# One group of the output projection in each chunk of the next round

## The chip, the cores and the metric

The kernel runs on one core of one Trainium2 chip. The metric is the time of one execution in microseconds of the device, as the median of several runs. The engines named below are TensorE (PE, with its weight loads as PEld), VectorE (DVE), ScalarE (ACT), GpSimd (POOL) and SyncE (SP), which only issues transfers.

## The reference, cut to what matters

The whole program is a decoder-like stack of two layers, each an attention part and a feed-forward part, every part followed by a sum with its input and a layer norm. The change is in the first part alone, a chunked linear attention with decay over 2 sequences of 1024 tokens, width 512, 16 heads of 32:

```python
q, k, v = silu(x @ Wq), silu(x @ Wk), silu(x @ Wv)     # split into 16 heads of 32
def step(S, inp):                                      # one chunk of 128 tokens
    scores = einsum('bchd,bshd->bhcs', qb, kb) * D
    o_intra = einsum('bhcs,bshd->bchd', scores, vb)
    o_inter = einsum('bchd,bhde->bche', qb, S) * q_decay
    S_new = chunk_decay * S + einsum('bshd,bshe->bhde', kb * k_decay, vb)
    return S_new, o_intra + o_inter
o = o * sigmoid((x @ Wg1) @ Wg2)
o = head_rmsnorm(o) * norm_w
x = layernorm(x + o @ Wo)
```

The last line's `o @ Wo` is the output projection ("wo" in the kernel), and `x + ...` the addition that goes with it.

## The kernel before, in words

Features lie on partitions, 4 pieces of 128, and tokens along the free axis. The 2048 tokens are cut into tiles of 512 (`TT`), a tile into four chunks of 128 (`CPT` = 4). The attention phase is five rounds: rounds t = 0 to 3 take tile t, and a tail round finishes tile 3. Every engine has its own program, a loop of `body(rd)` over the rounds, and the programs meet only at semaphores, so the order of the code within each engine is the order of its work.

A product in full precision is three matmuls in a reduced format: weights and data are split into a high part (a rounding copy, by ScalarE) and a low part (the rest, by GpSimd or VectorE), and `three_passes` (L111 to L113) multiplies high by high, high by low and low by high. A projection group of 128 output features over 512 tokens (`project`) is 4 x 3 = 12 matmuls into one of two PSUM banks (`proj`). The groups of all rounds stand in the lists `FIRST`, `SECOND`, `NEXT` and `TAIL`; `s_pj` counts finished groups, and `taken` says which engine has to have read the group two places before.

TensorE's round t: (from t = 2 the mean of an older tile, `mean_parts`, L369, which waits for the additions of tile t - 1 to x), then q (4 groups), `transform(0)` (L407, a step of the transform of the feed-forward weights, which waits for GpSimd's butterflies), the head norms of the tile before (L395), k, the gate's first product (L417), v, the gate (L520), `transform(1)`, four transposes of k (L525), the output projection of the tile BEFORE (`outputs`), and last the four chunks. In a chunk: `scores_of` (L430, 16 matmuls of 32 rows), `from_state` (L445, 16 of 32 x 32 into `o_ps`), `state_update` (L454, 16 of 32 columns into `u_ps`), `from_chunk` (L464, 16 of 32 columns into `o_ps`). `from_chunk(c)` waits until VectorE has masked the four score banks (`s_pr`), and `from_state(c + 1)` until VectorE has gated chunk c (`s_og`).

VectorE's round ends with four reads of the transposes (L858), four additions of the projection to x (`add_outputs`, L824), and for each chunk: four maskings (L868), the state (L872, four small instructions) and the gating (L877).

Three things hang on the last group of the output projection:

- The projection's inputs `onh` and `onl` are the buffers `xh` and `xl`, which hold the high and low part of the tile's x in the next round. So ScalarE's next round begins with

```python
act.wait_ge(s_pj, rd.base)
act.copy(xh[:, :, :], x[:, :, tok(t)]).then_inc(s_xh, 1)     # L629
```

  where `rd.base` is the number of all groups of the rounds before, the last `wo` among them.
- GpSimd's next round waits for that copy (`pool.wait_ge(s_xh, rd.t + 1)`), makes the four low parts (L739), then the low parts of three blocks of later weights (`blocks_low`, L719, behind ScalarE's L579), then eight butterflies (L732, L733). TensorE's q waits for all four low parts (`pe.wait_ge(s_xl, KD * t + 1)`), and `transform(0)` for the butterflies (`s_bf`).
- In the tail round ScalarE makes the high parts of the first feed-forward tile after the same count (`ffn_x_high`, L638), then two of weights (L632) and two blocks; GpSimd follows with the low parts of the data (L749) and of the weights (L753). TensorE's tail begins with `first_ffn_chunk(0)` (12 matmuls), which waits for them (`joint.lo13`, `joint.xl`), and goes on with the head norms, `first_ffn_chunk(1)` and the output projection of tile 3.

SyncE stores the blocks as GpSimd finishes them (L305) and loads the next ones (L300). The second phase of the kernel begins when all engines have left the block of the first.

Of the kernel before, what the change touches and what calls it, by code (L numbers as in the profile page):

```python
# [26 lines left out]
ALU = mybir.AluOpType  # L27
# [4 lines left out]
KD = D // P  # L32
# [72 lines left out]
def tok(t):  # L105
    return slice(t * TT, (t + 1) * TT)
# [9 lines left out]
def attention_phase(nc, joint, w13a, en, cn, w13b, w13x, x_dram, aw_d, ld_tok, ld_feat, ld_cols, wg1_d, wg2_d, nw_d, w2n, w2h):  # L116
# [6 lines left out]
    with ExitStack() as ctx:  # L123
# [4 lines left out]
        x, qT, aw_hi, aw_lo = joint.x, joint.first, joint.hi, joint.lo  # L128
# [25 lines left out]
        onh, onl = xh, xl  # L154
# [17 lines left out]
        s_pj = p.sem("proj_done")  # L172
# [11 lines left out]
        s_oh, s_ol = p.sem("on_hi"), p.sem("on_lo")  # L184
# [73 lines left out]
        with nc.Block() as block:  # L258
# [83 lines left out]
            def _(pe):  # L342
                def body(rd):
# [9 lines left out]
                    def project(name, w, m, hi, lo, ready=None):  # L353
                        out = bank(name, m)
                        for k in range(KD):
                            if ready is not None:
                                for sem, value in ready(k):
                                    pe.wait_ge(sem, value)
                            mm = three_passes(pe, out, aw_hi[:, w, k, m * P:(m + 1) * P],
                                              aw_lo[:, w, k, m * P:(m + 1) * P],  # L360
                                              hi[:, k, :], lo[:, k, :], k == 0, k == KD - 1)
                        mm.then_inc(s_pj, 1)
# [31 lines left out]
                                pe.wait_ge(*by_piece(m, s_sq, NT, p_sq))  # L394
                            pe.matmul(bank("norm", m), const[:, C_HEAD:C_HEAD + P], sq[:, m, :]).then_inc(s_pj, 1)  # L395

                    def outputs():
                        for m in range(KD):
                            project("wo", 3, m, onh, onl, (lambda k: [(s_ol, KD * rd.prev + k + 1)]) if m == 0 else None)

                    def transform(i):

# [45 lines left out]
                    def state_update(c):  # L448

                        pe.wait_ge(*rd.out("kT", c))  # L450
                        for m in range(KD):
                            for j in range(HPT):
                                hs = slice((m * HPT + j) * HD, (m * HPT + j + 1) * HD)
                                mm = pe.matmul(u_ps[j * HD:(j + 1) * HD, m, :], kd[:, c, hs], v[:, c, hs],  # L454
                                               tile_position=(0, j * HD))
                        mm.then_inc(s_u, 1)
# [22 lines left out]
                    if rd.tail:  # L479
                        first_ffn_chunk(0)  # L480
                        norms()
                        first_ffn_chunk(1)
                        outputs()
                        return
                    if rd.norms_x:
                        mean_parts()
# [35 lines left out]
                    for c in range(CPT):  # L522
# [2 lines left out]
                            mm = pe.transpose(out[:, m * P:(m + 1) * P], kT[:, m, c * CH:(c + 1) * CH],  # L525
                                              const[:, C_ID:C_ID + P])
                        mm.then_inc(s_pj, 1)
                    if not rd.first:
                        outputs()
                    scores_of(0)  # L530
                    for c in range(CPT):
                        from_state(c)
                        state_update(c)
                        from_chunk(c)
                        if c + 1 < CPT:
                            scores_of(c + 1)
# [221 lines left out]
            def _(dve):  # L758
# [28 lines left out]
                def body(rd):  # L787
                    t = rd.t

                    def norm_heads():  # L790

                        dve.wait_ge(s_og, CPT * t)
                        for m in range(KD):
                            dve.wait_ge(s_sd, KD * rd.prev + m + 1)
                            dve.scalar_tensor_tensor(out=on[:, m], in0=og[:, m, :], scalar=nw[:, m:m + 1],
                                                     in1=sq[:, m], op0=ALU.mult, op1=ALU.mult).then_inc(s_on, 1)

                    def centre_x():

                        dve.wait_ge(s_pj, rd.done("mb"))  # L800
                        for k in range(KD):
                            xt = x[:, k, tok(t - 2)]
                            dve.tensor_tensor(xt, xt, rd.bank("mb"), ALU.subtract)\
                               .then_inc(s_dt if k == KD - 1 else s_lc, 1)

                    def scale_x():

                        dve.wait_ge(s_lr, t - 1)
                        for k in range(KD):
                            xt = x[:, k, tok(t - 2)]  # L810
                            dve.tensor_tensor(xt, xt, lsq[:, 0], ALU.mult).then_inc(s_ln, 1)

                    def low_of_normed():

                        for k in range(KD):
                            dve.wait_ge(s_oh, KD * rd.prev + k + 1)
                            dve.tensor_tensor(onl[:, k], on[:, k], onh[:, k].bitcast(F32), ALU.subtract).then_inc(s_ol, 1)

                    def add_outputs():

                        for m in range(KD):
                            dve.wait_ge(s_pj, rd.done("wo", m))
                            xt = x[:, m, tok(rd.prev)]
                            dve.tensor_tensor(xt, xt, rd.bank("wo", m), ALU.add).then_inc(s_dt, 1)  # L824

                    if rd.tail:
                        norm_heads()
                        low_of_normed()
                        dve.wait_ge(joint.th, 1)
                        dve.scalar_tensor_tensor(out=ffn_sg, in0=ffn_sg, scalar=1.0, in1=joint.gate[:, :],  # L830
                                                 op0=ALU.add, op1=ALU.mult).then_inc(joint.sg, 1)
                        add_outputs()
                        return
                    if rd.norms_x:
                        centre_x()
                    dve.wait_ge(*rd.out("q", KD - 1))
                    dve.tensor_tensor(qd[:, :, :].rearrange("p m (c i) -> p m c i", c=CPT),
                                      qT[:, :, :].rearrange("p m (c i) -> p m c i", c=CPT),
                                      qdec[:, :, :].unsqueeze(2).to_broadcast([P, KD, CPT, CH]),
                                      ALU.mult).then_inc(s_qd, 1)  # L840

                    if not rd.first:
                        dve.wait_ge(s_st, (CPT + 1) * t)
                    dve.tensor_tensor(st[:, :, :].rearrange("p m c -> p (m c)").bitcast(I32),
                                      st[:, :, :].rearrange("p m c -> p (m c)").bitcast(I32),
                                      live[:, t:t + 1].to_broadcast([P, KD * HD]),
                                      ALU.bitwise_and).then_inc(s_st, 1)
                    if not rd.first:
                        norm_heads()
                    if rd.norms_x:  # L850
                        scale_x()
                    if not rd.first:
                        low_of_normed()
                    if rd.norms_x:
                        dve.wait_ge(s_ln, KD * (t - 1))
                    for c in range(CPT):
                        dve.wait_ge(s_pj, rd.done("kT", c))
                        dve.tensor_tensor(kd[:, c, :], rd.bank("kT", c), kdec[:, :], ALU.mult)\  # L858
                           .then_inc(s_dt, 1)
                    if not rd.first:  # L860
                        add_outputs()
                    dve.wait_ge(*rd.out("gate", KD - 1))
                    dve.wait_ge(s_st, (CPT + 1) * t + 1)
                    for c in range(CPT):
                        n = CPT * t + c
                        for j in range(HPT):
                            dve.wait_ge(s_sc, HPT * n + j + 1)
                            dve.tensor_tensor(pr[:, j], scores[j], dmask[:, j], ALU.mult).then_inc(s_pr, 1)  # L868

                        dve.wait_ge(s_u, n + 1)  # L870
                        for m in range(KD):
                            mm = dve.scalar_tensor_tensor(out=st[:, m], in0=st[:, m], scalar=cdec[:, m:m + 1],  # L872
                                                          in1=u_ps[:, m], op0=ALU.mult, op1=ALU.add)
                        mm.then_inc(s_st, 1)
                        dve.wait_ge(s_o, n + 1)
                        gated = sig[:, :, c * CH:(c + 1) * CH]
                        dve.scalar_tensor_tensor(out=gated, in0=gated, scalar=1.0, in1=o_ps[:, :, :],  # L877
                                                 op0=ALU.add, op1=ALU.mult).then_inc(s_og, 1)
                        dve.wait_ge(s_st, n + t + 2)
# [1137 lines left out]
```

## Time and profile before

| | |
|---|---|
| time of the kernel, median of 3 runs | 1880.44 us (1876.88 to 1881.67) |
| profiled execution, span from the first to the last instruction | 1871.9 us (its time as a run is not recorded apart; the median lies 8.5 us above the span) |
| busy | PE 1753.7 us (94%), PEld 1149.7 (61%), DVE 1323.0 (71%), ACT 982.2 (52%), POOL 1284.0 (69%) |
| attention phase | from 0 to about 360 us |
| an addition of the projection to x (L824, x16) | 686/689/689 ns (min/median/max) |
| loads of blocks after the chunks of round 1 (L300) | start at 156.03 us; ScalarE takes them from 191.10 (L579); 3.7 us each to landing |
| granted clock at 0.50 | seven stretches in which TensorE works; the shortest from 21.5 to 24.9 us, after 2.37 us without a matmul. In the one from 585.63, 512-column matmuls step 0.427 us (590.30, 590.73, 591.16). At 371 to 377 us the clock is 1.00 |

How to read it: times are from the span's start. A matmul's record is longer than its step, since matmuls are pipelined; steps are read from start to start. A row of a timeline has start, length, engine, line and operation, output and inputs, the count of instructions merged into it, and in brackets the idle time of the engine before it and what ended that. "issue" is time in which the engine waited for nothing that the profile shows. A row of the windows has the stretch, its length, then the busy time of PE, PEld, DVE, ACT and POOL with their instructions, the granted TensorE clock as a share of 2.4 GHz, the share of the DMA engines and GB/s.

### The profile page before, as it was taken

Reading aid. Unit: us, or ns where it says so; the run is one execution under the profiler, and the core shown is the slowest. Engines: PE = TensorE matmul, PEld = TensorE weight load, DVE = VectorE, ACT = ScalarE, POOL = GpSimd, SP = SyncE. Lnnn points to the kernel's source line nnn. Section 1 sums busy time; section 2 is a strip of 40 time slices with the busy share of each in tenths; the row PEclk is TensorE's granted clock in tenths of the full one; section 3 lists DMA queues with packets and bytes.
Section 4 is the critical chain, followed back from the end, with each engine's and each line's share of the span. In section 5 each row is a group of like instructions: output and inputs, shape, how many; then the busy total and the mean of one; then the engine's idle time right before and its main releaser. Section 6 shows DMA issues by size and latency. Waiting matters only on the chain. (4 is left out here: it accounts for less than half of the span.)

```text
span 1871.9 us, 27455 instructions
## 1 busy us (share of the span) xinstructions
PE 1753.7 (94%) x9472; PEld 1149.7 (61%) x9472; DVE 1323.0 (71%) x1532; ACT 982.2 (52%) x1686; POOL 1284.0 (69%) x992
## 2 busy tenths in 40 slices
PE   7898989799998999999899999999999999999998
PEld 5666666577755655555555556555556565667886
DVE  2424343433249989899998999899999999993322
ACT  5343443567465656755666556655554555543212
POOL 4533445166448998798987998798988798983111
PEclk9999999999999999999999999999999999999999
DMA  7442323588758888798787987686878687874662
GB/s 247 131 139 82 124 80 124 185 289 271 268 190 280 300 267 278 234 297 285 238 265 228 316 272 255 232 279 226 272 249 284 225 274 252 291 252 158 204 195 96
DMA packets 159226, 427.32 MB, mean 228 GB/s; under 512 B 30992, under 2 KB 54096, under 8 KB 158704
## 3 DMA queue, kind: packets, MB, share of 16 engines
q1 hardware_dynamic: 159088, 425.57, 68.7%
q8 instruction: 76, 1.25, 0.3%
q14 instruction: 62, 0.51, 0.1%
HBM read 356.30 MB, written 69.21 MB: 227 GB/s over the span
## 5 line engine op out<-in xcount | busy, mean ns | idle before, releaser
L1647 ACT ACTIVATE decay<-delta_on_states,a_neg 128x512 f32<-128x512 f32 x512 | 354.4, 692 | 339.3 <-DVE h_states L1803 338.2
L1898 POOL TENSOR_TENSOR q_or_raw_or_h_times_c<-h_states,c_rep 128x512 f32<-128x512 f32 x293 | 382.7, 1318 | 58.7 <-PE scan_y L1470 29.9
L1898 POOL TENSOR_TENSOR h_times_c_rest<-h_states,c_rep 128x512 f32<-128x512 f32 x219 | 283.5, 1304 | 36.0 <-DVE h_states L1803 17.9
L1864 POOL TENSOR_TENSOR h_lo<-v_or_silu_in_h_lo,h_hi 128x512 fp32r<-128x512 f32 x128 | 169.1, 1321 | 176.1 <-ACT h_hi L1545 172.3
L1803 DVE TENSOR_TENSOR_SCAN h_states<-decay,h_last,d_b 128x512 f32<-128x512 f32 x192 | 242.3, 1274 | 5.9 <-ACT decay L1647 1.1
L1803 DVE TENSOR_TENSOR_SCAN h_states<-decay,d_b 128x512 f32<-128x512 f32 x192 | 230.8, 1214 | 5.5 <-ACT decay L1647 1.2
L111 PE MATMUL y_or_aux<-h_hi,w 128*128 128x512 f32 x468 | 208.2, 445 | 5.8 <-POOL h_lo L1864 4.8
L1461 PE MATMUL du_spread<-stack,selectors 96*128 96x512 bf16 x512 | 159.0, 390 | 46.7 <-DVE d_b L1772 30.1
L1729 DVE SCALAR_TENSOR_TENSOR v_or_silu_in_h_lo<-v_or_silu_in_h_lo,gate_or_scores 128x512 f32<-128x512 f32 x127 | 86.3, 680 | 145.6 <-ACT v_or_silu_in_h_lo L1541 145.2
L112 PE MATMUL y_or_aux<-h_lo,w 128*128 128x512 f32 x468 | 184.7, 395 | 0.0
L113 PE MATMUL y_or_aux<-h_hi,w 128*128 128x512 f32 x468 | 184.1, 393 | 0.0
L1889 POOL TENSOR_TENSOR d_b_by_pool<-du_copied,b_rep 128x512 f32<-128x512 f32 x128 | 171.4, 1340 | 8.0 <-ACT du_copied L1655 8.0
L1772 DVE TENSOR_TENSOR d_b<-du_spread,b_rep 128x1024 f32<-128x1024 f32 x128 | 153.7, 1201 | 13.0 <-PE du_spread L1461 12.5
L1470 PE MATMUL scan_y<-q_or_raw_or_h_times_c,sum_selectors 128*32 128x512 f32 x586 | 135.8, 608 | 0.0
L111 PEld LDWEIGHTS y_or_aux<-h_hi,w 128*128 128x128 f32 x468 | 89.0, 190 | 73.1 <-issue 35.4
L1545 ACT CAST h_hi<-v_or_silu_in_h_lo 128x512 fp32r<-128x512 f32 x128 | 78.7, 615 | 101.2 <-DVE v_or_silu_in_h_lo L1735 100.9
L1735 DVE SCALAR_TENSOR_TENSOR v_or_silu_in_h_lo<-v_or_silu_in_h_lo,up_or_scores 128x512 f32<-128x512 f32 x128 | 86.5, 676 | 60.8 <-PE up_or_scores L113 60.6
L1741 DVE TENSOR_TENSOR x<-x,y_or_aux 128x512 f32<-128x512 f32 x122 | 82.3, 675 | 64.7 <-PE y_or_aux L113 64.6
L719 POOL TENSOR_TENSOR w_presplit_hi_lo<-w_presplit_hi_lo 128x512 fp32r<-128x512 f32 x32 | 41.5, 1319 | 119.9 <-ACT w_presplit_hi_lo L579 119.9
L111 PE MATMUL gate_or_scores<-attn_w_hi_or_x_hi_w,attn_w_lo_or_x_lo_w 128*128 128x512 f32 x256 | 116.1, 454 | 1.3 <-DVE v_or_silu_in_h_lo L1729 1.2
L111 PE MATMUL gate_or_scores<-attn_w_hi_or_x_hi_w 128*128 128x512 f32 x256 | 115.0, 449 | 2.5 <-DVE v_or_silu_in_h_lo L1729 1.3
L1470 PE MATMUL scan_y<-h_times_c_rest,sum_selectors 128*32 128x512 f32 x438 | 115.6, 609 | 0.0
(255 smaller groups left out, 4174.1 us busy)
## 6 DMA issues: line engine op xcount, KB each, us to landing
delta_on_states<-delta SPq DMA_DIRECT2D x256, 512.0 KB, 5.3
w<-w_split SPq DMA_DIRECT2D x112, 512.0 KB, 5.2
attn_w_hi_or_x_hi_w<-w_split SPq DMA_DIRECT2D x112, 512.0 KB, 5.1
attn_w_lo_or_x_lo_w<-w_split SPq DMA_DIRECT2D x112, 512.0 KB, 5.2
w_split<-w_presplit_hi_lo SPq DMA_DIRECT2D x32, 512.0 KB, 3.5
w_presplit_hi_lo<-in_w13b SPq DMA_DIRECT2D x32, 256.0 KB, 3.7
w_split<-attn_w_hi_or_x_hi_w SPq DMA_DIRECT2D x8, 1024.0 KB, 7.2
w_split<-attn_w_lo_or_x_lo_w SPq DMA_DIRECT2D x8, 1024.0 KB, 6.7
```

Of the source, the lines that this page charges most:

```text
L111: pe.matmul(out, w_hi, x_hi, start=first, stop=False)
L112: pe.matmul(out, w_hi, x_lo, start=False, stop=False)
L113: return pe.matmul(out, w_lo, x_hi, start=False, stop=last)
L1461: pe.matmul(uu[:, input_bank(s)], sel[:, r, :], stk[:, o % 2, j]).then_inc(s_uu, 1)
L1470: mm = pe.matmul(yb[j * 32:(j + 1) * 32, :], ysel[:, r, :], hc[(s + j) % NC_], start=(r == 0), stop=(r == QB - 1), skip_group_check=True, ...
L1647: act.activation(da[:, s % ND], dring[:, s % NR], ACT.Exp, scale=a[:, column(s):column(s) + 1]).then_inc(s_da, 1)
L1735: dve.scalar_tensor_tensor(out=sg[:, idx % RH], in0=sg[:, idx % RH], scalar=0.5, in1=up[:, :], op0=ALU.mult, op1=ALU.mult).then_inc(s_h, 1)
L1772: dve.tensor_tensor(db[:, :, :], uu[:, :, :], brep[:, tile_of(s // SPO) % 2].unsqueeze(1).to_broadcast([P, 2, TT]), ALU.mult).then_inc(s_d ...
L1803: dve.tensor_tensor_scan(hs[:, s % NH], da[:, s % ND], data, initial, ALU.mult, ALU.add).then_inc(s_hs, 1)
L1864: pool.tensor_tensor(hl[:, idx % RH], sg[:, idx % RH], hh[:, idx % RH].bitcast(F32), ALU.subtract).then_inc(s_hl, 1)
L1889: pool.tensor_tensor(dp[:, quad % 2], us[:, quad % 2], brep[:, tile_of(JB * quad // SPO) % 2], ALU.mult).then_inc(s_dp, 1)
L1898: pool.tensor_tensor(hc[s % NC_], hs[:, s % NH], crep[:, tile_of(s // SPO) % 2], ALU.mult).then_inc(s_hc, 1)
```

## The change

The output projection of the tile before no longer stands as one block of 48 matmuls ahead of the chunks. In rounds 1 to 3 its group c stands in chunk c, between the state update and the output from the chunk. VectorE's addition of group c stands between the state and the gating of chunk c. The tail round keeps its order.

```diff
-                    def outputs():
-                        for m in range(KD):
-                            project("wo", 3, m, onh, onl, (lambda k: [(s_ol, KD * rd.prev + k + 1)]) if m == 0 else None)
+                    def output(m):
+                        project("wo", 3, m, onh, onl, (lambda k: [(s_ol, KD * rd.prev + k + 1)]) if m == 0 else None)
...
-                        outputs()
+                        for m in range(KD):
+                            output(m)
                         return
...
-                    if not rd.first:
-                        outputs()
                     scores_of(0)
                     for c in range(CPT):
                         from_state(c)
                         state_update(c)
+                        if not rd.first:
+                            output(c)
                         from_chunk(c)
                         if c + 1 < CPT:
                             scores_of(c + 1)
...
-                    def add_outputs():
-
-                        for m in range(KD):
-                            dve.wait_ge(s_pj, rd.done("wo", m))
-                            xt = x[:, m, tok(rd.prev)]
-                            dve.tensor_tensor(xt, xt, rd.bank("wo", m), ALU.add).then_inc(s_dt, 1)
+                    def add_output(m):
+                        dve.wait_ge(s_pj, rd.done("wo", m))
+                        xt = x[:, m, tok(rd.prev)]
+                        dve.tensor_tensor(xt, xt, rd.bank("wo", m), ALU.add).then_inc(s_dt, 1)
...
-                        add_outputs()
+                        for m in range(KD):
+                            add_output(m)
                         return
...
-                    if not rd.first:
-                        add_outputs()
...
                         mm.then_inc(s_st, 1)
+                        if not rd.first:
+                            add_output(c)
                         dve.wait_ge(s_o, n + 1)
```

## Rows read from the trace of the kernel before

**Rows 1.** Windows, the chunk stage of round 1.

```profile
145.00:165.00 20.00, 15.04 (x521) 11.88 (x521) 15.85 (x37) 3.41 (x4) 17.83 (x15) 1.00 0.35 121
```

**Rows 2.** Waits of the weight loads, rounds 1 to 3.

```profile
PEld o_ps L464 <- DVE probs L868: 16.1, 12, 1.4
```

**Rows 3.** Timeline of TensorE, round 1 to the start of round 2.

```profile
133.46 0.19 PEld L111 LDWEIGHTS proj<-attn_x_hi,attn_w_hi_or_x_hi_w 128*128 128x128 f32 x1 [0.31 <-DVE k_decayed L858]
...
144.53 0.39 PE L113 MATMUL proj<-attn_x_hi,attn_w_lo_or_x_lo_w 128*128 128x512 f32 x1
144.84 0.18 PEld L430 LDWEIGHTS gate_or_scores<-q_or_raw_or_h_times_c,kT 32*128 32x128 f32 x1 [0.36 <-issue]
...
148.68 0.81 PEld L464 LDWEIGHTS o_ps<-probs,v_or_silu_in_h_lo 128*32 128x32 f32 x32 [1.37 <-DVE probs L868]
149.69 0.18 PEld L430 LDWEIGHTS gate_or_scores<-q_or_raw_or_h_times_c,kT 32*128 32x128 f32 x1 [0.20 <-issue]
150.79 0.81 PEld L445 LDWEIGHTS o_ps<-q_decayed,state 32*32 32x32 f32 x32
151.79 0.35 PEld L454 LDWEIGHTS u_ps<-v_or_silu_in_h_lo,k_decayed 128*32 128x32 f32 x32 [0.20 <-issue]
153.49 0.81 PEld L464 LDWEIGHTS o_ps<-probs,v_or_silu_in_h_lo 128*32 128x32 f32 x32 [1.34 <-DVE probs L868]
...
163.90 0.24 PEld L369 LDWEIGHTS proj<-x,const 128*32 128x32 f32 x8
164.98 0.50 PE L111 MATMUL proj<-attn_x_hi,attn_w_hi_or_x_hi_w 128*128 128x512 f32 x1
...
177.25 1.98 PE L407 MATMUL proj<-had_a,const 128*128 128x512 f32 x4
```

**Rows 4.** Timeline of the weight loads: last transposes, rounds 0 and 1.

```profile
62.23 0.42 PEld L525 LDWEIGHTS proj<-const,kT 128*128 128x128 f32 x4 [0.39 <-DVE k_decayed L858]
62.81 0.18 PEld L430 LDWEIGHTS gate_or_scores<-q_or_raw_or_h_times_c,kT 32*128 32x128 f32 x1 [0.17 <-issue]
...
132.73 0.42 PEld L525 LDWEIGHTS proj<-const,kT 128*128 128x128 f32 x4 [0.29 <-DVE k_decayed L858]
```

**Rows 5.** Timelines of ScalarE, GpSimd and VectorE beside the chunks of round 1.

```profile
144.95 1.90 ACT L629 CAST attn_x_hi<-x 128x2048 fp32r<-128x2048 f32 x1 [11.94 <-PE proj L113]
...
146.93 5.01 POOL L739 TENSOR_TENSOR attn_x_lo<-x,attn_x_hi 128x512 fp32r<-128x512 f32 x4 [11.10 <-ACT attn_x_hi L629]
...
164.57 1.29 POOL L733 TENSOR_TENSOR had_a<-had_b 128x512 f32<-128x512 f32 x1
...
149.82 0.69 DVE L877 SCALAR_TENSOR_TENSOR gate_tanh_or_og<-gate_tanh_or_og,o_ps 128x512 f32<-128x512 f32 x1 [0.57 <-PE o_ps L464]
```

**Rows 6.** Timelines of ScalarE, GpSimd and TensorE, round 3 to the tail.

```profile
316.41 2.18 ACT L638 CAST attn_w_hi_or_x_hi_w<-x 128x512 fp32r<-128x512 f32 x4 [12.01 <-PE proj L113]
...
322.05 2.36 POOL L753 TENSOR_TENSOR attn_w_hi_or_x_hi_w<-had_a,attn_w_hi_or_x_hi_w 128x1024 fp32r<-128x1024 f32 x1
...
335.58 0.19 PEld L111 LDWEIGHTS gate_or_scores<-attn_w_hi_or_x_hi_w 128*128 128x128 f32 x1 [0.20 <-issue]
...
338.47 1.88 PE L395 MATMUL proj<-probs,const 128*128 128x512 f32 x4
...
339.94 1.26 ACT L601 ACTIVATE probs<-proj,const 128x512 f32<-128x512 f32 x2
...
340.77 1.96 PE L395 MATMUL proj<-probs,const 128*128 128x512 f32 x4 [0.42 <-ACT probs L601]
...
341.91 0.69 ACT L601 ACTIVATE probs<-proj,const 128x512 f32<-128x512 f32 x1 [0.70 <-PE proj L395]
```

**Rows 7.** Timeline of TensorE after long idle times in the second phase.

```profile
371.33 1.13 PE L1404 MATMUL y_or_aux<-soft_in_x_hi,sum_weights_eps 128*32 128x512 f32 x3 [3.17 <-ACT soft_in_x_hi L1584]
...
585.63 1.03 PE L1461 MATMUL du_spread<-stack,selectors 96*128 96x512 bf16 x2 [4.24 <-DVE d_b L1772]
...
591.56 0.39 PE L111 MATMUL gate_or_scores<-attn_w_hi_or_x_hi_w 128*128 128x512 f32 x1
```

## The prediction

> **What bounds the kernel now.** I read the windows by stage first. In the chunk stage of round 1 TensorE is busy 15.04 of 20 us and VectorE 15.85, neither full [rows 1]. The list of waits says on what: in twelve chunks the output from the chunk (L464) waited 16.1 us, at most 1.4 at a time, for VectorE's masked scores (L868) [rows 2]. That hole is what the change would fill.
>
> The timeline of TensorE gives the length of every step [rows 3]. Rounds are numbered by their tile, t = 0 to 3, and round 1 is the pattern for 2 and 3. The output projection starts at 133.46 and its last matmul at 144.53; the scores follow at 144.84. A chunk goes scores 149.69, from the state 150.79, state update 151.79, output from the chunk 153.49: 4.81 us after the one before it at 148.68, with 1.34 idle before L464. The chunks end at 163.90, where the next round's mean parts begin, and q starts at 164.98.
>
> The timelines of ScalarE, GpSimd and VectorE show what is hidden now [rows 5]. The last projection group also releases ScalarE's copy of the next tile's high part (144.95, L629, 1.90 us), since that copy overwrites the buffer the projection reads (onh is xh). GpSimd's four low parts follow (146.93 + 5.01 = 151.94), then three blocks and eight butterflies, the last ending at 164.57 + 1.29 = 165.86. The next q needs the low parts at 164.98, 13.0 us after they are there; transform(0), at 177.25 [rows 3], needs the butterflies, 11.4 us after they are there. All that cover is the chunks. So I ask first what becomes late when the last group moves behind the fourth chunk's state update.
>
> **The change, part by part.** Nothing is added or removed in instructions: per round t = 1 to 3, 48 matmuls of projection and four VectorE additions (0.69 us each, the table above) move. The tail round keeps its order.
>
> *TensorE's chunk.* Scores to from-state 1.10, to state update 1.00, its weight loads 0.35. Then output(c) is new: 0.20 idle at the switch, as before L111 at 335.58, which also follows matmuls of 32 columns [rows 6]; first to second matmul 0.34, then ten steps of 0.233 (133.46 to 144.53 is 47 steps, 11.07 us, of which 46 at 0.233), so 0.20 + 0.34 + 2.33 = 2.87, and 0.31 from the last matmul to the next stage (144.53 to 144.84) [rows 3]. That is 3.18. The output from the chunk to the next scores is 1.01. Sum 1.10 + 1.00 + 0.35 + 3.18 + 1.01 = 6.64 us against 4.81. VectorE no longer ends any wait: the masked scores are ready 3.80 us after the scores start, TensorE gets to L464 after 5.63. VectorE's work of a chunk is at most 15.85 / 4 = 4.0 us [rows 1], with the addition 4.7, below 6.64. The near edge is another: the gating (149.82, 1.14 after L464's start at 148.68, and 0.69 long [rows 5]) ends 1.83 after L464 starts; the next from-state comes at 2.11. The addition put before it runs from 0.11 to 0.80 after L464's start and doesn't touch it.
>
> The Trainium skill (TensorEngine Tiling (Array Packing), section Tiling Modes, key properties) says that a change of tiling mode drains TensorE. The change puts two more such switches into each chunk, where update and output from the chunk now share a mode. The rows give it about 0.2 us a switch; were it free, the period would be about 6.4.
>
> *Start of the stage.* Scores(0) now follow the transposes of k. Round 0 has that order: last four transposes at 62.23, scores at 62.81, so 0.58 [rows 4]; from 132.73 that gives 133.31, 0.15 before the projection started [rows 3].
>
> *TensorE alone.* L464 of chunk 3 starts at 133.31 + 4 × 6.64 − 1.01 = 158.86, the mean parts 0.80 later at 159.66, against 163.90: 4.2 us gained in each of three rounds. The waits alone would say 12.7 us.
>
> *What is late next.* The last projection matmul starts 0.31 before L464, and ScalarE sees it 0.42 later (144.53 to 144.95): 158.97 in place of 144.95, 14.02 later. Everything hanging on it moves by that:
> - q of the next round: low parts 6.99 after the copy starts, so q at 158.97 + 7.04 = 166.01 against 164.98, 1.03 later, though the mean parts end near 160.7. TensorE stands idle some 5.2 us.
> - transform(0): butterflies end 20.91 after the copy starts, 179.88; with 0.05 to TensorE 179.93 against 177.25, 2.68 later. GpSimd's blocks also wait for ScalarE's blocks, which are right behind the copy as now.
> - SyncE's stores of these blocks and the loads behind them also move by 14; those loads start at 156.03 and are used at 191.10 (both in the table above), and land in 3.7 us, so some 17 us are left.
>
> Rounds 2 and 3 start so; each loses 2.68 by GpSimd's chain alone.
>
> *The tail.* There the last group releases ScalarE's copies for the first feed-forward chunk (316.41, L638), and through GpSimd the low part of the first weights, ready at 322.05 + 2.36 = 324.41, 8.00 after. TensorE takes it at 335.58, 19.17 after [rows 6]. Now it starts at 14.02 + 8.05 = 22.07 after the old release, 2.90 later, having idled 7 us. Behind it stand the head norms: L395 at 338.47, and ScalarE's logarithm at 339.94, which today waits for its own table, as a fresh norm takes only 1.14 (340.77 to 341.91). So 0.33 is given back: 2.57.
>
> Sum with TensorE at full clock: 2 × 2.68 + 2.57 = 7.9 us.
>
> *The clock.* Three idle stretches of 5.2, 5.2 and 7 us are new on TensorE. In this trace, after 4.24 us idle the granted clock was 0.50 (1.2 GHz): matmuls of 512 columns then step 0.427 (table above) in place of 0.233, from 585.63 to 591.56 [rows 7]; that stretch cost 5.93 × (1 − 0.233/0.427) = 2.7 us. The shortest stretch in the table above is 3.4 us, which costs 1.6 us. After 3.17 us idle, at 371.33, the clock held. For stretches of 5 and 7 us the nearest row is the 4.24. I take 2.2 between 1.6 and 2.7. In rounds 2 and 3, q then ends 1.03 + 2.2 = 3.2 late, more than the butterflies' 2.7, so 3.2 counts, not the sum. In the tail it lies on the path: 2.57 + 2.2 = 4.8. Total 2 × 3.2 + 4.8 = 11.2 us.
>
> The Trainium skill (TensorE: Matmul & The Clock Gate, Part 1) says "the default state is throttled, and activity releases the throttle". By it all three stretches cost; by the row at 371.33 none would, and the sum stays 7.9.
>
> After the tail both phases meet at the end of the block, and the second phase has its own loads and buffers, so I see nothing there that gives the delay back.
>
> The span is 1871.9 and the median 1880.44, 8.5 above; I take that as constant. 1880.44 + 11.2 = 1891.6, **1892 us**.
>
> **The rivals.**
> - *The clock holds* (0.2): 7.9 us, 1888.3. For it speaks 371.33, against it the 4.24 us row.
> - *Cheap switches too* (0.14): each output(c) without 0.2 to 0.25 of switch moves the last release 1.0 us earlier in three rounds. With the clock held, 7.9 − 3 = 5, 1885.4: within the measurement's limit.
> - *VectorE joins* (0.08): if the addition ran into the gating and both came after L464's end, 1.14 + 0.69 + 0.69 = 2.52 against 2.11, 0.41 per chunk, twelve times, 4.9: 1897. The 0.34 us between addition and gating speaks against.
> - *Faster* (0.05): the splitting of the next tile doesn't gate q, and TensorE's own 3 × 4.2 = 12.7 us come through: 1867.7. It decides when the low parts are there no later than TensorE, that is when the copy starts at 152.7 or before. In the code it can't start before the fourth group, near 159. For gain at all in rounds 2 and 3 it would need the butterflies by 177.2, that is the fourth group 2.7 us earlier than I make it.
> - The forecast itself: 0.53.
>
> **How the numbers follow.** Below 0.3% (5.6 us) either way a measurement can't tell this kernel from no change: 1874.8 to 1886.1. Slower takes the forecast, the held clock and VectorE: 0.81; same takes the cheap switches: 0.14; faster 0.05. Range: low end 1885.4 less some 1.5 for the spread of the runs (1876.9 to 1881.7), 1884; high end with 2.7 for the clock, 2 × 3.7 + 5.3 = 12.7, plus VectorE's 4.9, 1898.
>
> **What would show it.** L464's wait for L868 gone in rounds 1 to 3 and the chunk's period 6.6 us; L629 starting near 159 and q near 166, idle 5 us before its L111 and released by GpSimd's L739; L407 waiting for L733; in the tail L111 released by L753 after 7 us; granted clock 0.5 after each of these. Wrong if q starts without a wait, if the period is well off 6.6, or if the clock stays at 1.00 throughout.

## The result and the profile after

| | before | after |
|---|---|---|
| median of 10 runs | 1876.86 us (1873.90 to 1881.67) | 1886.22 us (1880.91 to 1892.84) |
| span of the profiled execution | 1871.9 us | 1885.1 us |
| mean granted clock | 0.991 | 0.983 |

The ratio is 1.005, with a 95% interval of 1.0034 to 1.0066: the change makes the kernel 9.4 us slower. The forecast's sum was 11.2 us.

The timeline of TensorE after, first chunks of round 1 and the way into round 2. L429, L453, L463 and L406 are the L430, L454, L464 and L407 of [rows 3].

```profile
132.40 0.18 PEld L429 LDWEIGHTS gate_or_scores<-q_or_raw_or_h_times_c,kT 32*128 32x128 f32 x1 [0.17 <-issue]
134.51 0.35 PEld L453 LDWEIGHTS u_ps<-v_or_silu_in_h_lo,k_decayed 128*32 128x32 f32 x32 [0.20 <-issue]
134.90 0.50 PE L111 MATMUL proj<-attn_x_hi,attn_w_hi_or_x_hi_w 128*128 128x512 f32 x1
...
137.90 0.81 PEld L463 LDWEIGHTS o_ps<-probs,v_or_silu_in_h_lo 128*32 128x32 f32 x32 [0.36 <-issue]
138.91 0.18 PEld L429 LDWEIGHTS gate_or_scores<-q_or_raw_or_h_times_c,kT 32*128 32x128 f32 x1 [0.20 <-issue]
...
157.39 0.81 PEld L463 LDWEIGHTS o_ps<-probs,v_or_silu_in_h_lo 128*32 128x32 f32 x32 [0.36 <-issue]
164.48 0.29 PEld L111 LDWEIGHTS proj<-attn_x_hi,attn_w_hi_or_x_hi_w 128*128 128x128 f32 x1 [5.99 <-POOL attn_x_lo L739]
...
179.43 1.98 PE L406 MATMUL proj<-had_a,const 128*128 128x512 f32 x4
```

The hole in the chunk is gone: L463 waits for nothing that the profile names, where L464 waited 1.34 us for the masked scores [rows 3]. A chunk now takes 6.50 us (138.91 − 132.40; the L463 of the next chunk, at 144.39, gives the same from 137.90) against 4.81. The new wait stands at the end: 5.99 us of TensorE's weight loads idle before q, until GpSimd's low parts (L739).

The waits of the weight loads over rounds 1 to 3 and the tail say the same in three lines (us in total, times, longest):

```profile
PEld proj L111 <- POOL attn_x_lo L739: 12.0, 2, 6.0
...
PEld gate_or_scores L111 <- POOL attn_w_hi_or_x_hi_w L753: 7.3, 1, 7.3
PEld o_ps L463 <- issue: 4.4, 12, 0.4
```

19.3 us of waits for GpSimd stand where 16.1 us of waits for VectorE stood [rows 2]. The last of them is in the tail, in TensorE's timeline:

```profile
343.02 0.79 PE L111 MATMUL gate_or_scores<-attn_w_hi_or_x_hi_w 128*128 128x512 f32 x1 [7.03 <-POOL attn_w_hi_or_x_hi_w L753]
348.13 3.84 PE L395 MATMUL proj<-probs,const 128*128 128x512 f32 x8
```

The timelines of ScalarE and GpSimd show what GpSimd waited for (compare [rows 5]):

```profile
157.50 1.90 ACT L629 CAST attn_x_hi<-x 128x2048 fp32r<-128x2048 f32 x1 [25.41 <-PE proj L113]
...
159.48 4.95 POOL L739 TENSOR_TENSOR attn_x_lo<-x,attn_x_hi 128x512 fp32r<-128x512 f32 x4 [24.60 <-ACT attn_x_hi L629]
164.40 3.73 POOL L719 TENSOR_TENSOR w_presplit_hi_lo<-w_presplit_hi_lo 128x512 fp32r<-128x512 f32 x3
...
177.16 1.31 POOL L733 TENSOR_TENSOR had_a<-had_b 128x512 f32<-128x512 f32 x1
```

The copy starts at 157.50, right after the last projection group, and not at 144.95; ScalarE idled 25.4 us before it. The low parts are there at 164.43, and q starts at 164.48.

VectorE's timeline in the first chunk shows that the moved addition (L822) and the gating (L876) don't meet:

```profile
138.01 0.69 DVE L822 TENSOR_TENSOR x<-x,proj 128x512 f32<-128x512 f32 x1 [1.20 <-PE proj L113]
139.05 0.69 DVE L876 SCALAR_TENSOR_TENSOR gate_tanh_or_og<-gate_tanh_or_og,o_ps 128x512 f32<-128x512 f32 x1 [0.35 <-PE o_ps L463]
```

Last the clock, from the windows (the stretch, its length, busy time of PE, PEld, DVE, ACT, POOL, then the granted clock):

```profile
166.00:168.00 2.00, 2.00 (x6) 1.59 (x5) 0.00 (x0) 0.00 (x0) 2.00 (x2) 0.50 0.77 307
168.00:170.00 2.00, 2.00 (x6) 1.55 (x5) 0.00 (x0) 0.00 (x0) 2.00 (x3) 0.50 1.01 403
...
344.00:346.00 2.00, 2.00 (x6) 1.57 (x5) 0.00 (x0) 0.00 (x0) 2.00 (x2) 0.50 1.00 399
358.00:360.00 2.00, 2.00 (x7) 1.56 (x6) 1.19 (x2) 0.75 (x2) 0.00 (x0) 0.53 0.00 0
```

From 163.6 to 170.4 us TensorE has 1.2 GHz, and again from 252.3 to 259.1, 341.0 to 347.9 and 358.1 to 361.5 (read from windows of 1 us). Before had no such stretch between its first 26 us and the end of the attention phase while TensorE worked.

**One measure for all runs.** The second phase, untouched, took between 1508 and 1522 us (span less the start of the last addition) in the profiled runs, so a median wanders by a few us for reasons that aren't the change's. Beside the ratio I read three lengths from each trace: round 2 and round 3, each from the start of the last transposes of k before it (L525) to the next such start, and the tail stage, from there in round 3 to the start of the last addition. The last transposes are the last four of sixteen weight loads; in e1, e6, e8 and e10 a slow stretch makes the timeline merge them with the four before them, and the start is still that of the thirteenth.

| kernel | median us | ratio to before (95%) | round 2 | round 3 | tail stage |
|---|---|---|---|---|---|
| before | 1876.86 | | 85.65 | 85.74 | 54.95 |
| the change | 1886.22 | 1.005 (1.0034 to 1.0066) | 88.76 | 88.76 | 60.52 |
| e1 late release, projection as before | 1896.61 | 1.0085 (1.0057 to 1.0114) | 90.23 | 91.46 | 62.97 |
| e2 two groups ahead | 1870.88 | 0.9967 (0.9946 to 0.9988) | 83.40 | 83.49 | 54.24 |
| e3 busy matmuls | 1882.44 | 1.0028 (1.0006 to 1.0049) | 88.05 | 88.03 | 58.42 |
| e4 butterflies first | 1884.23 | 1.0031 (1.001 to 1.0052) | 88.31 | 88.51 | 60.39 |
| e5 tail released early | 1874.73 | 1.0 (0.998 to 1.0019) | 87.88 | 87.88 | 53.00 |
| e6 = e3 + e4 | 1880.59 | 1.0023 (1.0006 to 1.0041) | 86.21 | 86.26 | 59.74 |
| e7 pieces | 1871.39 | 0.9961 (0.994 to 0.9983) | 82.80 | 82.81 | 52.42 |
| e8 pieces, one ahead, tail early | 1868.65 | 0.9959 (0.994 to 0.9978) | 83.44 | 82.37 | 51.58 |
| e9 chain edits alone, on before | 1876.13 | 0.9993 (0.9971 to 1.0016) | 85.66 | 85.74 | 56.11 |
| e10 = e7 + e5 | 1867.25 | 0.9951 (0.993 to 0.9972) | 82.85 | 84.12 | 50.09 |

The ratios are against the runs of before made with each group of kernels (medians 1875.78 for e1 to e4, 1876.21 for e5 to e8, 1879.27 for e9 and e10). By the lengths the change costs 3.1 + 3.0 + 5.6 = 11.7 us in the first phase. Round 1 is in none of the three lengths: from the last transposes of round 0 to its own it took 70.50 us before and with the change.

### The profile page after: what moved, and what is told of

It is laid out like the page before. It is cut to its first block and busy times, and to the rows that moved or that the text cites. A ratio compares the mean times of both kernels' runs of the same rounds, so it can differ in the third digit from the quotient of the medians.

```text
span 1885.1 us, 27455 instructions
## 1 busy us (share of the span) xinstructions
PE 1765.1 (94%) x9472; PEld 1154.9 (61%) x9472; DVE 1328.3 (70%) x1532; ACT 981.4 (52%) x1686; POOL 1285.1 (68%) x992
## 3 DMA queue, kind: packets, MB, share of 16 engines
q8 instruction: 76, 1.25, 0.3%
## 5 line engine op out<-in xcount | busy, mean ns | idle before, releaser
L111 PE MATMUL y_or_aux<-h_hi,w 128*128 128x512 f32 x468 | 207.3, 443 | 6.5 <-POOL h_lo L1863 5.6
L111 PEld LDWEIGHTS y_or_aux<-h_hi,w 128*128 128x128 f32 x468 | 88.4, 189 | 73.3 <-issue 34.6
L111 PE MATMUL gate_or_scores<-attn_w_hi_or_x_hi_w 128*128 128x512 f32 x256 | 116.2, 454 | 9.5 <-POOL attn_w_hi_or_x_hi_w L753 7.0
L111 PE MATMUL gate_or_scores<-attn_w_hi_or_x_hi_w,attn_w_lo_or_x_lo_w 128*128 128x512 f32 x256 | 116.0, 453 | 0.8 <-DVE v_or_silu_in_h_lo L1728 0.7
L111 PE MATMUL up_or_scores<-attn_w_hi_or_x_hi_w 128*128 128x512 f32 x256 | 115.0, 449 | 0.0
```

Of the source, the lines that this page charges most:

```text
L111: pe.matmul(out, w_hi, x_hi, start=first, stop=False)
```

## The experiments

Theory A is the prediction's: the release of ScalarE's copy moves behind the chunks, and what hangs on it is late. Theory B puts the loss on the chunks themselves (length, switches, additions). The others stand with their runs.

**e1, the late release alone.** On the kernel before, for both copies:

```diff
                         act.wait_ge(s_pj, rd.base)
+                        act.wait_ge(s_sc, HPT * CPT * t)
                         act.copy(xh[:, :, :], x[:, :, tok(t)]).then_inc(s_xh, 1)
...
                         act.wait_ge(s_pj, rd.base)
+                        act.wait_ge(s_sc, HPT * CPT * NT)
                         act.wait_ge(s_ln, KD)
```

> The kernel before, with its projection as one block; only the next tile's copy to the high part (L629, and L638 before the tail) waits in addition for the last scores of the chunk stage. Theory A (the late release of the copy makes the loss): in the rows of before the last scores are done near 160.6, 15.6 us after the copy's present start, so q comes 160.6 + 7.04 = 167.6 in place of 165.0, transform(0) 181.5 in place of 177.25, 4.3 us per round in rounds 2 and 3; the tail's first feed-forward chunk 15.6 + 8.05 - 19.17 = 4.5 later, with some 2 us of slower clock. Sum some 14 us above before. Theory B (the longer chunk, its mode switches and its additions make the loss): nothing in the chunks changes, so the time of before within 0.3%.

Rounds 2 and 3 grew by 4.6 and 5.7 us, the tail stage by 8.0, with every matmul and addition in its old place. The waits of TensorE's weight loads, from round 0 to the tail:

```profile
PEld proj L111 <- POOL attn_x_lo L741: 11.0, 3, 3.8
...
PEld gate_or_scores L111 <- POOL attn_w_hi_or_x_hi_w L755: 4.8, 1, 4.8
```

Three waits before q, not two: my edit also held the copy of round 1, which the change leaves alone, and this expectation overlooked it. That round grew by 6.3 us (76.82 in place of 70.50 from the last transposes of round 0 to its own). Without it the first phase lost 18.3 us, against 14 expected and far from B's nothing; the median is 20.8 us above before. In its trace the clock is at 0.50 at each q, also at 227 to 231 and 371 to 374 us, and from 354 to 361 in the tail; the expectation had only the last.

**e2, half the groups.**

```diff
+                    if not rd.first:
+                        output(0)
+                        output(1)
                     scores_of(0)
...
-                        if not rd.first:
-                            output(c)
+                        if not rd.first and c < 2:
+                            output(c + 2)
```

and the same for the additions.

> The change for half of the groups: groups 0 and 1 stand ahead of the chunks, group 2 in chunk 0 and group 3 in chunk 1, additions likewise. Theory A: the last group ends some 6.3 us later than before, which the 11.4 us of room at transform(0) and the 13.0 us at q cover, so only the gain is left: 5.6 us of projection less in front, 2 x 1.7 us more in the chunks, 2.2 us per round, 6.6 us under before. Theory B: groups in chunks cost by themselves, so half of the change costs about half of what the change costs, 4 to 5 us above before.

Rounds are 2.25 us shorter than before each, as A has it, and the kernel is faster than before by 0.33%. A group in chunk 0 or 1, in the place that the change gives it, is a gain when the release is early enough. The kernel is 4.9 us under before, where 6.6 was expected. The tail stage gained 0.7 and not 2.2; it has a slow stretch from 340.1 to 343.5.

**e3, the clock held.** Ahead of the wait for the low parts, into the bank that q's group 0 overwrites; in the tail 28 of them into the gate's bank:

```diff
+                    def keep_busy(out, count):
+                        for _ in range(count):
+                            pe.matmul(out, aw_hi[:, 1, 0, 0:P], aw_hi[:, 1, 0, :])
...
+                    if rd.norms_x:
+                        keep_busy(bank("q", 0), 20)
                     if not rd.first:
                         pe.wait_ge(s_xl, KD * t + 1)
```

> The changed kernel with 20 matmuls of 512 columns added on TensorE ahead of its wait for the low parts in rounds 2 and 3, and 28 ahead of the tail's first feed-forward chunk, into banks that are overwritten next. They fill the idle time and nothing waits for them. Theory A with the clock's part: the granted clock stays at 1.00, q takes 2.7 us less, of which the butterflies let 0.9 through in each of rounds 2 and 3; the tail is 2.7 us shorter. 4 to 5 us under the changed kernel. Theory C (the clock is no part of the loss): the time of the changed kernel or more.

Two windows and a wait of its trace show the two halves of the answer:

```profile
157.00:171.00 14.00, 13.54 (x88) 9.64 (x83) 1.41 (x3) 6.93 (x8) 11.98 (x10) 1.00 0.32 118
336.00:347.00 11.00, 10.39 (x40) 6.92 (x39) 0.00 (x0) 6.92 (x11) 9.96 (x7) 1.00 0.79 301
```

```profile
PE proj L406 <- POOL had_a L740: 3.3, 2, 1.6
```

The clock held in all three places, and then the butterflies, hidden in the change itself, ended the wait at transform(0), 1.6 us each time. So a round got back 0.7 of the 2.7 us, the tail stage 2.1. The median is 3.8 us under the change's, just short of the 4 to 5 expected.

**e4, the butterflies.** `butterflies(2 * rd.t)` stands first in GpSimd's round, ahead of its wait for the copy.

> The changed kernel with GpSimd's eight butterflies of each round moved ahead of its wait for the copy to the high part, so that they run beside the chunks and transform(0) doesn't wait for them. Theory A as the trace after shows it (butterflies end 1.0 us before TensorE comes to transform(0), because q runs at half clock): no difference, within 1 us of the changed kernel. Theory D (the butterflies end the wait, as the prediction's sum without the clock has it): up to 2.7 us per round, 5 us under the changed kernel.

A round gained 0.25 to 0.45 us. The wait for the butterflies was no part of the change's loss by itself, so D, which had up to 2.7 us a round, falls. The median is 2.0 us under the change's, within the scatter of the runs.

**e6, both at once.**

> The two edits of e3 and e4 together in the changed kernel. Theory A with both bounds: with the clock held, only the low parts bound q, 0.4 us later than before, so a round takes some 86.2 us against 88.8 of the changed kernel, 88.0 with the busy matmuls alone and 88.4 with the butterflies alone; with the tail's 2 us, 7 us under the changed kernel, more than the 3.8 and 2.0 of the two edits added. If the two bounds don't stand side by side, the gains only add: 5.8 us or less.

Rounds of 86.21 and 86.26 us: 2.5 us less than the change, where the single edits gave 0.7 and 0.35. Two bounds of nearly equal height stand side by side, and only removing both shows either. What is left over before is 0.5 to 0.6 us; the low parts' own lateness is 0.4 of it. The median alone, 5.6 us under the change's, would not have told this from gains that add. The tail stage stayed at 59.74, with two slow stretches (304.4 to 307.9 and 352.2 to 355.6) where e3's has one.

**e5, the tail.**

```diff
                     def ffn_x_high():
-                        act.wait_ge(s_pj, rd.base)
+                        act.wait_ge(s_pj, ROUNDS[NT - 1].done("v", CPT - 1))
```

> The changed kernel with one wait exchanged: ScalarE's copies for the first feed-forward chunk (L638), which overwrite the high part of Wq and not the projection's inputs, wait for round 3's last v group in place of its last projection group. Rounds 1 to 3 are untouched. Theory A: the tail's chain (copies, GpSimd's low parts, first weights) is over before the chunks are, the 7.3 us of idle time and the slow clock behind it go, and the tail stage, last transposes to last addition, falls from 60.5 us to 51 to 52, so 9 us under the changed kernel and near the time of before. Theory B (chunks, switches and additions make the loss): the tail stage keeps its 60.5 us, since all of these stay.

One wait exchanged: the tail stage fell from 60.52 to 53.00 us, below before's 54.95, and the kernel is back at the time of before. B's items are all still there. Of the 11.5 us between the medians of the change and e5 the tail is 7.5; 1.8 more are the two rounds (87.88 each), which the edit doesn't touch and whose slow stretches are shorter in this trace. The timeline of ScalarE shows the copy out of the way (316.41 in [rows 6], 335.01 with the change):

```profile
308.60 2.17 ACT L638 CAST attn_w_hi_or_x_hi_w<-x 128x512 fp32r<-128x512 f32 x4
```

**e7, the chain cut short.**

```diff
-                        act.copy(xh[:, :, :], x[:, :, tok(t)]).then_inc(s_xh, 1)
+                        for k in range(KD):
+                            act.copy(xh[:, k], x[:, k, tok(t)]).then_inc(s_xh, 1)
...
-                        pool.wait_ge(s_xh, rd.t + 1)
+                        blocks_low(beside_chunks(rd.t))
                         for k in range(KD):
+                            pool.wait_ge(s_xh, KD * (rd.t - 1) + k + 2)
...
-                        pe.wait_ge(s_xl, KD * t + 1)
...
+                                (lambda k: [(s_xl, KD * (t - 1) + k + 2)]) if m == 0 else None)
```

with `blocks_high(beside_chunks(t))` ahead of the copy, the butterflies as in e4, and in the tail the weights and blocks ahead of the data on ScalarE and GpSimd.

> The changed kernel with its order on TensorE and VectorE kept, and the chain behind the last group cut short: ScalarE copies the high part in four pieces, GpSimd makes each low part as its piece comes, TensorE's first q group waits for piece after piece, and the blocks and butterflies (in the tail the weights and blocks) stand ahead of the copy on ScalarE and GpSimd. Theory A: q's first group ends some 6.4 us after the last projection group, worth 3.0 us per round against before, and the tail some 3; in all 9 us under before, 18 under the changed kernel. Theory B: no more than the 2 us that the butterflies alone gave.

The change's order of matmuls and additions is kept whole, and the rounds are 2.9 us shorter than before, 6.0 shorter than with the change. TensorE's timeline around the first q group:

```profile
159.35 1.06 PE L369 MATMUL proj<-x,const 128*32 128x512 f32 x8
160.65 0.47 PE L111 MATMUL proj<-attn_x_hi,attn_w_hi_or_x_hi_w 128*128 128x512 f32 x1 [0.24 <-POOL attn_x_lo L741]
...
161.81 0.50 PE L111 MATMUL proj<-attn_x_hi,attn_w_hi_or_x_hi_w 128*128 128x512 f32 x1 [0.22 <-POOL attn_x_lo L741]
...
163.06 0.50 PE L111 MATMUL proj<-attn_x_hi,attn_w_hi_or_x_hi_w 128*128 128x512 f32 x1 [0.29 <-POOL attn_x_lo L741]
...
164.32 0.50 PE L111 MATMUL proj<-attn_x_hi,attn_w_hi_or_x_hi_w 128*128 128x512 f32 x1 [0.29 <-POOL attn_x_lo L741]
```

TensorE steps at GpSimd's pace, 1.25 us a piece, with idle times of 0.2 to 0.3 and no slow clock between 130 and 390 us. With the tail's 2.5 the three lengths give 8.3 us, near the 9 expected; the median is only 4.8 us under before. Round 1 took 71.47 us, 1.0 more than before, and the second phase was long in this trace (1519 us); the rest isn't assigned.

**e9, the control.** The edits of e7 on the kernel before.

> The kernel before, its projection as one block, with the chain edits of e7 alone (pieces, blocks, butterflies and weights ahead of the copy). Theory A: before, the chain had 11 us and more of room, so shortening it gives nothing: rounds of 85.7 us, tail 55, the time of before within 0.3%; e7's gain is then the projection's place, let through. Theory E (the chain edits are worth something by themselves): 5 us or more under before.

Rounds of 85.66 and 85.74 us, those of before to 0.01. In rounds 2 and 3 the chain was free before; the gain of e7 is the projection's place, let through. Round 1 shows a price of the chain edits: it took 71.35 us, 0.85 more. The blocks now stand ahead of the copy and wait for their loads, so the copy starts at 75.22 us in place of 62.92, and q waits for the low parts. The tail stage is 1.2 us longer, in a trace with a slow stretch from 305.2 to 308.6.

**e8 and e10, the best versions.** In e8 group 0 stands ahead of the chunks in rounds 1 and 2; e10 has all groups in the chunks.

> The edits of e7, with group 0 ahead of the chunks and one group in each of chunks 0 to 2 in rounds 1 and 2, all four in the chunks in round 3, and the tail's copies released as in e5. Theory A: a chunk without a group after the last one hides the rest of the split; each group in a chunk gains 2.8 - 1.7 = 1.1 us, 3.3 us in each of rounds 1 and 2 and 4 in round 3: rounds of 82.4 us, tail 51; 10.5 us under before, the lowest of all. Theory B: no lower than e2.

> e7 with the tail's copies released as in e5, all four groups in the chunks of all three rounds. Theory A: rounds as in e7, 82.8 us, tail as in e8, 51.6: within 1 us of e8 on the first phase, about 1868 to 1870 us. If a group ahead of the chunks is worth having (as e8 was built), it is slower than e8 by 1 us or more.

A round without a slow stretch is 82.37 us in e8 (round 3) and 82.80 in e7, whose rounds 2 and 3 e10 has too. So a group ahead of the chunks is worth 0.4 us a round. TensorE's timeline of e8 shows why: q follows the mean parts without a wait, where in e7 it waits 0.2 to 0.3 us for each of the four pieces. The price is the old wait for the masked scores, 1.23 us, in the one chunk without a group.

```profile
161.79 1.04 PE L369 MATMUL proj<-x,const 128*32 128x512 f32 x8
162.77 0.50 PE L111 MATMUL proj<-attn_x_hi,attn_w_hi_or_x_hi_w 128*128 128x512 f32 x1
```

e8's reason held, at its forecast of 82.4, and so did e10's forecast of 82.8. Which of the two is faster the medians can't tell: the difference is 0.9 us in two rounds, less than their scatter and than what slow stretches add. One from 132.2 to 135.6 lies in e8's round 2 (1.1 us more), one from 337.0 to 340.4 in its tail, one from 214.5 to 217.9 mostly in e10's round 3 (1.3 us more), and e10's tail has none. e10 has the lowest median, 1867.25 us, 0.49% under before (0.9951, 0.993 to 0.9972), and 1.0% under the change; between e7, e8 and e10 the intervals overlap.

## Why the prediction was right

Both sides of the sum are counted from the last transposes of round 1, which came 0.9 us earlier in the profile after.

- **The time**, 1891.6 us: 1886.22, near the low end of the range. Of the 5.4 us between them 3.6 are the start: the sum was put on 1880.44, the median of three runs, and ten runs gave 1876.86. The 8.5 us between span and median are no constant either: in every run of the record that has both, time and span are 1.7 to 1.9 us apart, so the profiled execution before was a quick one. The increase is 9.4 us by the medians and 11.7 by the lengths, for a sum of 11.2. That the lengths come so near is in part luck: 1.6 of them are a slow stretch that no term foresaw.
- **TensorE's chunk**, 6.64 us: 6.50. The term that was off is the first switch: L111 starts 0.04 us after the update's last weight load (134.51 + 0.35 to 134.90), not 0.20. The second switch was as read, 0.33 from the start of the last matmul (137.57). That VectorE ends no wait held, addition at 0.11 and gating at 1.15 after L463's start, as forecast.
- **TensorE alone**, 4.2 us gained per round: 4.7. The mean parts start 26.50 us after the last transposes (158.31) in place of 31.17; the shorter chunk again.
- **The last release**, 14.02 us later: from the transposes 25.69 in place of 12.22, 13.47 later, the shorter chunk four times.
- **q**, 1.03 us later: 32.67 in place of 32.25, 0.42.
- **The clock**, 2.2 us a stretch: q to transform(0) took 14.95 us in place of 12.27, 2.7; in the tail, 343.02 to 348.13 in place of 335.58 to 338.47, 2.2. The two misses in a round, q earlier and the clock dearer than said, cancel by luck: transform(0) is 3.1 us late for 3.2.
- **The butterflies**, 2.7 us, under the 3.2: they ended at 178.47, 0.96 before transform(0), and alone would have made it 2.2 late. e3 showed them as the next bound, e6 the two together.
- **The tail**, 4.8 us: 5.6. Its feed-forward chunk was 2.2 late for 2.90 (release again), the clock there as said. Not foreseen was the fourth slow stretch, at 358 us, in the tail's own output projection: the logarithm was 4.0 late (2.2 and 2.2, less 0.4 given back), the last addition 5.6; the 1.6 between them are that stretch.
- **The second phase** gave nothing back and took nothing that can be told from its own scatter.

Of the rivals, the held clock was wrong in all three places: the granted clock was 0.50 after each. The Trainium skill (TensorE: Matmul & The Clock Gate, Part 1) says that the throttled clock is the default and that activity lifts it. By it the clock would fall in all three, and this trace agrees. The cheap switches were half right (one of two was nearly free), VectorE took no part. The switch from 32 columns to 128 showed 0.04 us from the last weight load to the next matmul, the other way some 0.1 over a normal step of 0.233. By the Trainium skill (TensorEngine Tiling (Array Packing), Tiling Modes) both drain TensorE; the 0.04 us leave next to nothing for it. The faster rival was named with its point, a copy that needn't wait for the fourth group. e5 is that case, in the tail alone. e7 and e10 keep the wait and shorten what follows it; there 2.9 us per round came through of what TensorE gains by itself, and 3.4 in e8's round 3, where three of four groups are in the chunks.

What stays open are the slow stretches that follow no long idle time (below). A separate buffer for the projection's inputs, which would undo the release alone in rounds 2 and 3, wasn't tried; it needs 16 KB more per partition, two buffers of 4 x 512 numbers of 4 bytes. e1 tests that release from the other side.

## What to carry to other kernels

Filling a hole on one engine moves the ends of what is moved. Ask for the last instruction of the moved work who waits for its count, buffers that it reads included, and walk that chain to its consumer with the room it has now; here a release 13.5 us later met 11.4 and 13.0 us of room, and 11.2 in the tail. A hole filled by part of the work, or a chain that is shortened and handed over in pieces, turned the same move from a loss of 0.5% into a gain of 0.3 to 0.5%. And when two bounds are close, test them together: alone each looked like a third of a microsecond to 0.7, both gave 2.5.

## What the runs showed of the hardware that was not expected

- The granted clock fell to 0.50 for 3 to 4 us in places where TensorE's order and its waits are those of before, which held 1.00: at 358 us after 2.12 us idle in the profile after (the same 2.12 at 347.60 before), and in e6, e8, e9 and e10 around or after the transposes of k, with no idle time above 1.4 us in e8. Where its cost can be read it is 1.1 to 1.6 us, and what decides it is open. In e1 the clock fell at q after 2.69 us idle.
- After a long idle time the clock stayed at 1.00 for a while and fell later: in the tail TensorE idled from 336.0, and the record shows 1.00 until 341.0.
- A slow stretch after 5 us of idle lasted 7 us in the change's rounds and some 3 us in e5's, with the same instructions; the rounds differ by 0.9 us (88.76 and 87.88).
